# The second LayerNorm of token groups 1 to 3 moved behind attention, and transposed values copied in pairs on ScalarE

## The chip, the cores and the metric

The kernel runs on one core of one Trainium2 chip. The metric is the device time of one execution in microseconds (us); for the kernel before, three runs gave 694.21, 695.79 and 697.62, and their median is the time to compare with. The profile is that of one further execution.

## The reference

The input x is 16 batches of 128 rows of 512. It is first changed by cross-attention to a context of the same shape, then by a feed-forward with routed experts, each behind a LayerNorm over the 512 columns:

```
def _layernorm(x, axis=-1, eps=1e-05):
    m = jnp.mean(x, axis=axis, keepdims=True)
    v = jnp.var(x, axis=axis, keepdims=True)
    return (x - m) / jnp.sqrt(v + eps)
...
qk = jnp.einsum('bhdq,bhdl->bhql', qh, kh) * scale        # 8 heads of 16 rows, 512 x 512 scores
sm = jax.nn.softmax(qk, axis=-1)
ret = jnp.einsum('bhql,bhdl->bhdq', sm, vh)
...
x = x + jnp.tanh(g_xattn[0]) * xattn(_layernorm(x), ctx_2048, ctx_2048, gamma)
x = x + jnp.tanh(g_ffn[0]) * ffn(_layernorm(x), ...)
```

The feed-forward brings each of the 2048 rows down to 256 columns, picks two of eight experts by router logits on the same normalised row, adds a shared expert, goes back up to 512 columns and adds gelu(row) times a 512 x 512 core matrix. The second LayerNorm, in front of it, is the one that moves.

## The kernel before

**Attention** runs in windows, one batch begun in each. For every window TensorE computes the 512 x 512 scores of eight heads twice: once with queries on the partitions (`nat`, 16 pairs of products, from which VectorE takes row maxima with a 1.2 us reduction each, `mx`), and once with keys on the partitions (`ring`, three banks, from which ScalarE takes the exponentials, 32 instructions `P`). A small row of maxima per half of the heads is transposed and put back as one more row of the queries (`mrow`). TensorE then multiplies values and exponentials into `pv`; the value tile `VT` holds for each head 32 columns, 16 with the values and 16 with ones, so that the sums for the softmax come out of the same products. Even heads have the values first, odd heads the ones. ScalarE copies `pv` to `U` twice in a window, once per half of the heads. The values come from the context by four transposes into a ring bank, two to a bank; ScalarE copies each bank into VT with two instructions of 128 elements a partition, one for even and one for odd heads (line 661).

**After the products**, GpSimd separates numerator and denominator (lines 740 to 746), the denominator goes to memory and back (VectorE's `recip`), and GpSimd multiplies and adds the residual (`att`, `x1`, lines 750 and 754) in `ao`. One window later comes the second LayerNorm of that batch: VectorE's bn_stats and bn_aggr (`xstats`, `xaggr`, lines 698 and 702), placed after its ninth and tenth maxima; on GpSimd three small steps (`xnegm`, `xveps`, `xrstd`), the normalisation `u` into `un` (line 766), and `x1t`, which adds a constant row to x1 (line 769). SyncE stores `un` and `ao` to memory, and later loads four batches at once as a group.

**The feed-forward** handles four groups of four batches. The order on every engine is written out by hand, by `seq`. For group r TensorE transposes the normalised rows (`uT`), computes router logits (`lg`, `lt`), `h`, the token ranks (`rk`), transposes the halves of gelu(h) into rows (`rt`, from `gh` and its low part `gl`), transposes the gate table `Gp` (`gt`), and computes the core product of the group before (`core`), which stands between these. VectorE splits operands into high and low halves (`ul`, `gl`, `gul`), selects experts, and builds `Gp` from the chain csum, carry, rk, pk, slf, slots, gat, pk, Gp. ScalarE does the gelus and casts. GpSimd issues eight scatter DMAs a group (`sc`) and, from group 2 on, computes the first `gl`. An instruction waits behind all that stands before it on its engine. Four EH banks go round; a bank is free when its reader is done. The normalised rows lie in `XA` for groups 0, 1 and 3, in `u` for group 2. The last batches' LayerNorm (batch 15) runs as `last_stats` and `last_norm` inside the feed-forward.

Behind group 3 come the experts' blocks, TensorE products from end to end, and the sums.

## Time and profile before

| | |
|---|---|
| median of 3 runs | 695.79 us |
| the profiled execution | 693.51 us, of it the span 690.6 us |
| PE busy | 651.6 us, 94% of the span |
| ACT busy | 531.1 us, 77% |
| DVE busy | 515.6 us, 75% |
| POOL busy | 468.1 us, 68% |
| granted TensorE clock | full in all 40 slices |
| second LayerNorm, statistics (L698) | 16 of 680 ns |
| second LayerNorm, normalisation (L766) | 16 of 766 ns |
| value copies (L661) | 64 of 269 ns |

PE is TensorE, DVE VectorE, ACT ScalarE, POOL GpSimd, SP SyncE; L661 is line 661 of the kernel. Busy time overlaps between engines, and averages over stages with different limits, so what counts is which engine has no idle time in the stage that is changed. Of small pipelined instructions the start of the next may come before the end of the last; the pace is then the distance of starts and not the duration.

### The profile page before, as it was taken

The page shows a single profiled execution, that of the slowest core. Times are in us where ns is not written, and L with a number is a line of the kernel's source. Part 1 is how long each engine was busy: PE and PEld are TensorE (multiplying, and loading weights), DVE is VectorE, ACT ScalarE, POOL GpSimd, SP SyncE. Part 2 cuts the span into 40 slices and gives each one's busy share as a digit, 9 for nine tenths or more (in the row PEclk, how much of TensorE's full clock was granted, in tenths as well). Part 3 has the DMA queues.
Part 4 walks back from the last instruction along what each step waited for, and adds up shares of the span by engine and source line. Part 5 has one row for each costly group of instructions (what it writes and reads, how often), then busy time and mean ns, then how long its engine had stood idle before and what let it go on. Part 6 is the DMA issues. An engine that isn't in the chain of part 4 may idle for free.

```text
span 690.6 us, 18438 instructions
## 1 busy us (share of the span) xinstructions
PE 651.6 (94%) x6005; PEld 342.6 (50%) x6005; DVE 515.6 (75%) x859; ACT 531.1 (77%) x1125; POOL 468.1 (68%) x468
## 2 busy tenths in 40 slices
PE   1799999999999999999999999989999999999998
PEld 0122222222222222222345655579999998998744
DVE  3989999999999999999789877853444434444466
ACT  2389999999999999999888568567777776776411
POOL 3688898888888879986737443506756656665722
PEclk9999999999999999999999999999999999999999
DMA  6755776666767666656335653579988998696596
GB/s 195 249 168 195 221 242 199 194 187 189 221 197 228 198 180 202 190 173 210 113 123 170 228 190 123 171 166 173 125 146 116 127 130 109 99 122 91 61 299 252
DMA packets 128482, 120.40 MB, mean 174 GB/s; under 512 B 64132, under 2 KB 97668, under 8 KB 128392
## 3 DMA queue, kind: packets, MB, share of 16 engines
q1 hardware_dynamic: 114968, 104.09, 53.5%
q0 software_dynamic: 12192, 14.16, 13.7%
q8 instruction: 52, 0.85, 0.5%
q10 hardware_dynamic: 1232, 0.98, 0.5%
q14 instruction: 38, 0.31, 0.1%
HBM read 60.25 MB, written 49.10 MB: 158 GB/s over the span
## 4 chain that ended last, share of the span: by engine, by line
PE 65%; DMA 13%; POOL 11%; DVE 4%; ACT 3%; issue 2%; SPq 2%; POOLq 0%; DVEq 0%
PE EH L1333 23%; PE Y L1333 15%; PE pv L571 11%; PE ring L558 7%; PE nat L546 4%; DMA QS<-q_scratch 2%; DMA q_scratch<-qhl 2%; ACT P L642 2%; POOL wlo L812 1%; DMA u<-in_wall 1%; DMA rd<-den_scratch 1%; DMA QS<-mrow 1%; DMA k_scratch<-khl 1%; POOL y_sums L2235 1%; DMA x_rows<-ao 1%
## 5 line engine op out<-in xcount | busy, mean ns | idle before, releaser
L717 DVE TENSOR_REDUCE mx<-nat 128x2 f32<-128x1024 f32 x256 | 296.6, 1212 | 14.1 <-PE nat L546 13.8
L642 ACT ACTIVATE P<-ring 128x512 f32<-128x512 f32 x512 | 281.1, 601 | 16.8 <-PE ring L558 10.9
L2235 POOL DMA_INDIRECT y_sums<-ysb,to x74 | 124.8, 1687 | 81.6 <-DVE ysb L2165 62.5
L571 PE MATMUL pv<-P,VT 128*32 128x256 f32 x2048 | 157.6, 391 | 0.4
L546 PE MATMUL nat<-KS,QS 48*128 48x512 f16 x512 | 113.1, 394 | 20.2 <-DMA QS<-q_scratch 14.0
L558 PE MATMUL ring<-QS,KS 49*128 49x512 f16 x512 | 119.3, 391 | 9.1 <-ACT P L642 6.8
L1333 PE MATMUL EH<-XA,whi 128*128 128x256 f16 (+1 forms) x688 | 104.9, 258 | 0.5 <-DMA XA<-g_rows 0.5
L1333 PE MATMUL Y<-whi,u 128*128 x592 | 104.3, 273 | 0.2
L571 PEld LDWEIGHTS pv<-P,VT 128*32 128x32 f32 x2048 | 43.9, 108 | 99.1 <-issue 49.1
L2115 DVE TENSOR_TENSOR u<-X,u 128x512 f16<-128x512 f32 x62 | 42.7, 689 | 62.1 <-ACT u L1739 59.0
L558 PEld LDWEIGHTS ring<-QS,KS 49*128 49x128 f16 x512 | 30.7, 93 | 111.1 <-ACT P L642 88.5
L1333 PE MATMUL EH<-XA,wlo 128*128 128x256 f16 (+1 forms) x344 | 84.6, 258 | 0.0
L1333 PE MATMUL Y<-wlo,u 128*128 x296 | 80.7, 273 | 0.0
L1733 ACT ACTIVATE X<-EH,bcur 128x256 f32<-128x256 f32 x124 | 63.2, 560 | 15.7 <-PE EH L1333 8.6
L1333 PEld LDWEIGHTS EH<-XA,whi 128*128 x688 | 64.0, 98 | 7.1 <-issue 1.0
L1333 PEld LDWEIGHTS Y<-whi,u 128*128 128x128 f16 x592 | 57.9, 98 | 7.8 <-issue 1.2
L1739 ACT CAST u<-X 128x512 f16<-128x512 f32 x62 | 38.3, 618 | 5.2
L546 PEld LDWEIGHTS nat<-KS,QS 48*128 48x128 f16 x512 | 26.5, 95 | 29.2 <-issue 15.0
L1333 PEld LDWEIGHTS EH<-XA,wlo 128*128 x344 | 33.6, 98 | 2.8
L750 POOL TENSOR_TENSOR ao<-tn,rd 128x512 f32<-128x512 f32 x16 | 20.4, 1275 | 16.5 <-DMA rd<-den_scratch 16.4
L1333 PEld LDWEIGHTS Y<-wlo,u 128*128 128x128 f16 x296 | 28.9, 98 | 3.2
L1747 ACT CAST uh<-Y 128x256 f16<-128x256 f32 x16 | 6.0, 373 | 31.0 <-PE Y L1582 31.0
(282 smaller groups left out, 1039.2 us busy)
## 6 DMA issues: line engine op xcount, KB each, us to landing
QS<-q_scratch SPq DMA_DIRECT2D x64, 96.0 KB, 2.7
KS<-k_scratch SPq DMA_DIRECT2D x62, 96.0 KB, 2.3
u<-in_wall SPq DMA_DIRECT2D x7, 640.0 KB, 4.0
X<-in_x SPq DMA_DIRECT2D x16, 256.0 KB, 3.3
q_scratch<-qhl SPq DMA_DIRECT2D x16, 256.0 KB, 2.2
xr<-in_x SPq DMA_DIRECT2D x16, 256.0 KB, 3.5
rd<-den_scratch SPq DMA_DIRECT2D x16, 256.0 KB
u_rows<-un SPq DMA_DIRECT2D x16, 256.0 KB
```

The lines of the kernel that those rows point to most:

```text
L546: m = pe.matmul(nat[k % 2][:, a, :], QS[i][r, g, n, q0:q0 + P], KS[i][r, g, n, :], start=True, stop=True)
L558: pe.matmul(ring[place[key] % 3][:, :], KS[i][r, g, n, lb * P:lb * P + P], QS[i][r, g, n, :], start=True, stop=True).then_inc(t_ring.sem, 1)
L571: m = pe.matmul(pv[32 * j:32 * j + 32, q], VT[i][:, lb, g, j, :], Pb[4 * (s % 2) + j][:, q], start=(lb == 0 and half == 0), stop=(lb == 3) ...
L642: act.activation(Pb[4 * (s % 2) + j][:, :], bank[:, :], ACT.Exp).then_inc(t_use.sem, 1)
L717: dve.tensor_reduce(mx[:, k // 8, :, k % 8], nat[k % 2][:, :, :], AX.X, ALU.max).then_inc(t_max.sem, 1)
L750: done(pool.tensor_tensor(ao[i][:, :], tn[:, :], rd[:, :], ALU.mult))
L812: done(pool.tensor_tensor(wlo[:, cols], wst[i][:, 0:many], whi[:, cols], ALU.subtract))
L1333: m = pe.matmul(dst, l, r, start=first and n == 0, stop=last and n == 2, skip_group_check=skip)
L1733: m = act.activation(af[j % 2][:, tile, :], EH[j % 2][:, n, s * BLK:(s + 1) * BLK], ACT.Gelu, bias=bcur[:, j % 2, tile:tile + 1], scale=bc ...
L1739: act.copy(ah[j % 2][:, 2 * n:2 * n + 2, :], af[j % 2][:, 2 * n:2 * n + 2, :]).then_inc(t_ah.sem, 1)
L2115: dve.tensor_tensor(al[j % 2][:, 2 * n:2 * n + 2, :], af[j % 2][:, 2 * n:2 * n + 2, :], ah[j % 2][:, 2 * n:2 * n + 2, :], ALU.subtract).th ...
L2235: pool.indirect_dma_start(out=ysum[:, :], out_offset=bass.IndirectOffsetOnAxis(ap=to[:, j % 2, a:a + 1], axis=0), in_=ysb[j % 2][:, a, :], ...
```

## The change

It has two parts.

**Values.** VT becomes two stretches of 512 + 16 columns, one for even and one for odd heads. In both the values stand at the start of each 32 columns, with ones behind. The weights of an odd head are read from 16 columns further left, so that ones come first and values after; the first 16 of these lie in the spare columns at the end of the even stretch. One copy with the same pattern for both can then move a whole bank, 256 elements a partition.

**Second LayerNorm.** For batches 0 to 3 nothing changes. For batches 4 to 15 attention only computes x1 and the row with the constant added (which goes to `un` now); SyncE stores x1 itself where the normalised rows went. In the feed-forward VectorE takes statistics of a loaded group (four bn_stats, four bn_aggr) and GpSimd normalises it in place (three small steps on all four batches, four normalisations); TensorE waits for the normalisation of each batch before transposing it.

```diff
     def dve_small(w):
...
-               ([(w - 3, "xstats"), (w - 3, "xaggr")] if w >= 3 else []) + \
+               ([(w - 3, "xstats"), (w - 3, "xaggr")] if 3 <= w < 3 + G4 else []) + \
...
         if w >= 3:
-            jobs += [(w - 3, n) for n in ("xnegm", "xveps", "xrstd", "u", "x1t")]
+            if w < 3 + G4:
+                jobs += [(w - 3, n) for n in ("xnegm", "xveps", "xrstd", "u")]
+            jobs.append((w - 3, "x1t"))
...
-                ck.wait(t_pool, s, "u")
-                sp.dma_start(us[s], un[:, :]).then_inc(t_us.sem, 16)
+                ck.wait(t_pool, s, "u" if s < G4 else "x1")
+                sp.dma_start(us[s], un[:, :] if s < G4 else ao[s % 2][:, :]).then_inc(t_us.sem, 16)
...
-                        m = pe.matmul(pv[32 * j:32 * j + 32, q], VT[i][:, lb, g, j, :], Pb[4 * (s % 2) + j][:, q],
+                        m = pe.matmul(pv[32 * j:32 * j + 32, q], values(i, g, lb, j), Pb[4 * (s % 2) + j][:, q],
...
-                    src = bank[:, 0:2 * P].rearrange("p (l j g d) -> p l g j d", l=2, g=2, d=DH)
-                    for g in range(2):
-                        m = act.copy(VT[i][:, 2 * a:2 * a + 2, g, :, DH * g:DH * g + DH], src[:, :, g, :, :])
-                    m.then_inc(t_use.sem, 1)
+                    src = bank[:, 0:2 * P].rearrange("p (n g d) -> p n g d", g=2, d=DH)
+                    act.copy(value_rows[i][:, 2 * QUADS * a:2 * QUADS * a + 2 * QUADS, :, :], src).then_inc(t_use.sem, 1)
...
+        def row_stats(r):
+            wait(dve, t_uu[r % 2], r)
+            for t in range(G4):
+                if r > 1:
+                    wait(dve, t_mv, r - 1, t)
+                dve.bn_stats(sx[:, t, :], ub[r][:, t, :]).then_inc(t_sx.sem, 1)
+            for t in range(G4):
+                wait(dve, t_sx, r, t)
+                if t == 0 and r > 1:
+                    wait(dve, t_ln, r - 1, "veps")
+                dve.bn_aggr(mv[:, t, :], sx[:, t, :]).then_inc(t_mv.sem, 1)
...
+            row_stats(1)
...
-                    if o == (1, "r", "ms"):
-                        ends["late"]["vector"]()
+                    if o == (1, "gl", 1):
+                        row_stats(2)
+                    elif o == (0, "core", G4 - 1):
+                        row_stats(3)
...
+        def normed(r):
+            wait(pool, t_mv, r, G4 - 1)
...
+            for t in range(G4):
+                pool.tensor_scalar(ub[r][:, t, :], ub[r][:, t, :], ln[:, t, 0:1], ln[:, t, 2:3], ALU.add, ALU.mult).then_inc(t_nu.sem, 1)
...
+            normed(1)
...
                     elif o == (0, "sc", G4 - 1):
                         last_norm()
+                        normed(2)
+                    elif o == (1, "sc", G4 - 1):
+                        normed(3)
```

Three places in the feed-forward where the order changes. First VectorE at the first group's `gl`. Before:

```order
L1824 SCALAR_TENSOR_TENSOR red<-red 128x4
L698 BN_STATS statx<-ao 128x6
L702 BN_AGGR mvx<-statx 128x2
L2013 TENSOR_TENSOR gl<-gf,gh 128x512
L1857 TENSOR_SCALAR gat<-red 128x4
L1859 TENSOR_SCALAR gat<-red 128x4
L1865 TENSOR_TENSOR pk<-m,gat 128x32 x2
L1869 COPY Gp<-cst 128x4
L1875 TENSOR_TENSOR Gp<-pk 128x12x8
L2013 TENSOR_TENSOR gl<-gf,gh 128x512
```

And now (`ro` is the memory that holds the statistics, `XA` the rows of group 1):

```order
L1836 SCALAR_TENSOR_TENSOR red<-red 128x4
L2072 BN_STATS ro<-XA 128x6 x4
L2077 BN_AGGR mv<-ro 128x2 x4
L2025 TENSOR_TENSOR gl<-gf,gh 128x512
L1869 TENSOR_SCALAR gat<-red 128x4
L1871 TENSOR_SCALAR gat<-red 128x4
L1877 TENSOR_TENSOR pk<-m,gat 128x32 x2
L1881 COPY Gp<-cst 128x4
L1887 TENSOR_TENSOR Gp<-pk 128x12x8
L2025 TENSOR_TENSOR gl<-gf,gh 128x512
```

One bn_stats and one bn_aggr of batch 14 are replaced by four and four of group 1.

Then VectorE in group 1, from the second `gl` to the gates. Before:

```order
L1821 TENSOR_REDUCE red<-pp 128x4
L1824 SCALAR_TENSOR_TENSOR red<-red 128x4
L2013 TENSOR_TENSOR gl<-gf,gh 128x512
L1835 TENSOR_REDUCE csum<-msum 128x8
L1838 TENSOR_TENSOR carry<-carry,csum 128x8
L1841 TENSOR_TENSOR rk<-EH,cst 128x32
L1848 TENSOR_TENSOR pk<-rk,m 128x32 x2
L1851 TENSOR_REDUCE slf<-pk 128x8
L1854 CAST slots<-slf 128x8
L1857 TENSOR_SCALAR gat<-red 128x4
L1859 TENSOR_SCALAR gat<-red 128x4
L1865 TENSOR_TENSOR pk<-m,gat 128x32 x2
```

And now:

```order
L1833 TENSOR_REDUCE red<-pp 128x4
L1836 SCALAR_TENSOR_TENSOR red<-red 128x4
L2025 TENSOR_TENSOR gl<-gf,gh 128x512
L2072 BN_STATS ro<-u 128x6 x4
L2077 BN_AGGR mv<-ro 128x2 x4
L1847 TENSOR_REDUCE csum<-msum 128x8
L1850 TENSOR_TENSOR carry<-carry,csum 128x8
L1853 TENSOR_TENSOR rk<-EH,cst 128x32
L1860 TENSOR_TENSOR pk<-rk,m 128x32 x2
L1863 TENSOR_REDUCE slf<-pk 128x8
L1866 CAST slots<-slf 128x8
L1869 TENSOR_SCALAR gat<-red 128x4
```

The statistics of group 2 stand between `gl` and `csum`; those of batch 15, which stood some ten instructions further up, are gone.

Then GpSimd, from batch 15's LayerNorm to the first `gl` that it computes. Before:

```order
L2183 DMA g_rows<-XB,slots 17664x272 x4
L757 TENSOR_SCALAR lnx<-mvx 128x1
L759 TENSOR_SCALAR lnx<-mvx 128x1
L762 TENSOR_TENSOR lnx<-lnx,cst 128x1
L766 TENSOR_SCALAR un<-ao,lnx 128x512
L769 TENSOR_TENSOR ao<-ao,tb 128x512
L2183 DMA g_rows<-rows,slots 17664x272 x4
L2183 DMA g_rows<-acc,slots 17664x272 x4
L2192 TENSOR_TENSOR gl<-gf,gh 128x512
```

And now:

```order
L771 TENSOR_TENSOR un<-ao,tb 128x512
L2235 TENSOR_SCALAR ln<-mv 128x4
L2236 TENSOR_SCALAR ln<-mv 128x4
L2238 TENSOR_TENSOR ln<-ln,cst 128x4
L2241 TENSOR_SCALAR u<-u,ln 128x512 x4
L2208 DMA g_rows<-rows,slots 17664x272 x4
L2208 DMA g_rows<-acc,slots 17664x272 x4
L2235 TENSOR_SCALAR ln<-mv 128x4
L2236 TENSOR_SCALAR ln<-mv 128x4
L2238 TENSOR_TENSOR ln<-ln,cst 128x4
L2241 TENSOR_SCALAR XA<-XA,ln 128x512 x4
L2217 TENSOR_TENSOR gl<-gf,gh 128x512
```

Batch 15 keeps only its addition; group 2 is normalised ahead of the eight scatters of group 1, and group 3 between these and `gl` of group 2.

## Rows read from the trace of the kernel before

**Rows 1.** The head of the page.

```profile
span 690.6 us, 18438 instructions
```

**Rows 2.** Busy time by stretch; columns: stretch, then length, then us busy of each engine.

```profile
200.00:220.00 20.00, 19.53 (x202) 5.58 (x198) 19.76 (x23) 19.39 (x41) 17.89 (x23) 1.00 0.68 206
...
380.00:420.00 40.00, 40.00 (x257) 23.09 (x255) 29.77 (x97) 24.68 (x49) 17.58 (x19) 1.00 0.57 201
```

**Rows 3.** ScalarE in time, one attention window: start us, duration us, line, operation [idle before].

```profile
195.86 0.58 ACT L620 COPY U<-pv 128x512 f32<-128x512 f32 x1
...
200.88 0.43 ACT L661 COPY VT<-ring 128x128 f32<-128x128 f32 x2 [0.16 <-PE ring L590]
...
206.13 0.58 ACT L620 COPY U<-pv 128x512 f32<-128x512 f32 x1
...
209.77 6.14 ACT L642 ACTIVATE P<-ring 128x512 f32<-128x512 f32 x11 [0.15 <-PE ring L558]
215.81 0.58 ACT L620 COPY U<-pv 128x512 f32<-128x512 f32 x1
```

**Rows 4.** VectorE in time, the same window.

```profile
207.30 0.68 DVE L698 BATCH_NORM_STATS2 statx<-ao 128x6 f32<-128x512 f32 x1
...
209.01 0.17 DVE L702 BATCH_NORM_AGGREGATE mvx<-statx 128x2 f32<-128x6 f32 x1
```

**Rows 5.** ScalarE in time, an early window.

```profile
45.29 0.58 ACT L620 COPY U<-pv 128x512 f32<-128x512 f32 x1
...
54.97 0.58 ACT L620 COPY U<-pv 128x512 f32<-128x512 f32 x1
```

**Rows 6.** Groups by line and form, whole span; busy us, mean ns of one.

```profile
L620 ACT COPY U<-pv 128x512 f32<-128x512 f32 x32 | 18.6, 580 | 0.3 <-PE pv L571 0.3
...
L661 ACT COPY VT<-ring 128x128 f32<-128x128 f32 x64 | 13.9, 269 | 8.5 <-PE ring L590 8.5
...
L766 POOL TENSOR_SCALAR un<-ao,lnx 128x512 f32<-128x512 f32 x16 | 12.2, 766 | 1.8
```

**Rows 7.** Around the first group's gl: VectorE, then TensorE.

```profile
359.26 1.09 DVE L2013 TENSOR_TENSOR gl<-gf,gh 128x512 f16<-128x512 f32 x1 [0.42 <-ACT red L1648]
...
362.13 0.69 DVE L2013 TENSOR_TENSOR gl<-gf,gh 128x512 f16<-128x512 f32 x1
...
363.96 0.27 PE L1414 MATMUL Y<-id,gl 128*128 128x128 f16 x2
...
369.58 0.39 PE L1333 MATMUL EH<-gh,whi 128*128 128x512 f16 x1 [1.55 <-ACT uh L1608]
```

**Rows 8.** Before Gp of group 1: GpSimd, VectorE, TensorE.

```profile
381.09 0.25 POOL L757 TENSOR_SCALAR lnx<-mvx 128x1 f32<-128x1 f32 x1
...
382.41 0.78 POOL L766 TENSOR_SCALAR un<-ao,lnx 128x512 f32<-128x512 f32 x1
383.27 1.26 POOL L769 TENSOR_TENSOR ao<-ao,tb 128x512 f32<-128x512 f32 x1
...
383.34 1.35 DVE L1848 TENSOR_TENSOR pk<-rk,m 128x32 f32<-128x32 f32 x2
...
385.65 0.26 DVE L1875 TENSOR_TENSOR Gp<-pk 128x96 f32<-128x96 f32 x1
...
386.16 0.60 PE L1431 MATMUL EH<-cst,Gp 128*96 128x128 f32 x4
```

**Rows 9.** Around gl of group 2: GpSimd, VectorE, TensorE.

```profile
405.73 1.16 POOL L2192 TENSOR_TENSOR gl<-gf,gh 128x512 f16<-128x512 f32 x1
...
407.90 0.20 DVE L1835 TENSOR_REDUCE csum<-msum 128x8 f32<-128x32 f16 x1
...
408.44 0.29 DVE L1848 TENSOR_TENSOR pk<-rk,m 128x32 f32<-128x32 f32 x2
...
409.70 0.26 DVE L1875 TENSOR_TENSOR Gp<-pk 128x96 f32<-128x96 f32 x1
...
409.18 0.28 PE L1414 MATMUL Y<-id,gl 128*128 128x128 f16 x2
```

More of the change, by code:

```diff
@@ L196, in program @@
             "rbb": sb("rbb", [P, G4, E]), "tb": sb("tb", [P, L]), "lp": sb("lp", [P, L]),
+            "mv": sb("mv", [P, G4, 2]), "ln": sb("ln", [P, G4, 3]),
             "gb": sb("gb", [P, NT]), "zs": sb("zs", [P, LAT]), "Z": sb("Z", [P, LAT]),
@@ L233, in stacks @@
         if i:
-            A("gap", [P, 3, L])
+            A("gap", [P, 3 * L - 4 * DH])
         own = [A(f"{n}{i}", [P, 2, QUADS // 2, L], F16) for n in ("QS", "KS")]
-        return own + [A(f"VT{i}", [P, LB, 2, QUADS, 32])]
+        return own + [A(f"VT{i}", [P, 2, L + DH])]
     pair = [stacks(0)]
@@ L243, in attention @@
     QS, KS, VT = zip(*pair)
+    value_rows = [v[:, :, 0:L].rearrange("p g (n c) -> p n g c", c=32)[:, :, :, 0:DH] for v in VT]
+    values = lambda i, g, lb, j: VT[i][:, :, :].rearrange("p g c -> p (g c)")[:, L * g + 32 * (QUADS * lb + j):L * g + 32 * (QUADS * lb + j) + 32]
     mx = A("mx", [P, 2, 2, 8])
@@ L515, in last_x1 @@
             sp.wait_ge(t_pool.sem, t_pool.at[B - 1, "x1t"])
-            sp.dma_start(x1s[B - 1], ao[(B - 1) % 2][:, :]).then_inc(t_st.sem, 16)
+            sp.dma_start(x1s[B - 1], un[:, :]).then_inc(t_st.sem, 16)
         def last_u():
-            sp.wait_ge(t_pool.sem, t_pool.at[B - 1, "u"])
-            sp.dma_start(us[B - 1], un[:, :]).then_inc(t_us.sem, 16)
+            sp.wait_ge(t_pool.sem, t_pool.at[B - 1, "x1"])
+            sp.dma_start(us[B - 1], ao[(B - 1) % 2][:, :]).then_inc(t_us.sem, 16)
         late["sync"] = last_x1, last_u
@@ L722, in body @@
                 small(ck, *job)
-        def last_stats():
-            for what in ("xstats", "xaggr"):
-                small(Clock(dve), B - 1, what)
-        late["vector"] = last_stats
         over_windows(dve, body, tail)
@@ L741, in job @@
             elif what == "nb":
-                ck.wait(t_st, b - 2)
+                ck.wait(t_st if b - 2 < G4 else t_us, b - 2)
                 done(pool.tensor_scalar(ao[i][:, :], U[1][:, :], cme[:, 1:2], 1.0, ALU.mult, ALU.mult))
@@ L767, in job @@
             elif what == "x1t":
-                ck.wait(t_pool, b, "u")
-                done(pool.tensor_tensor(ao[i][:, :], ao[i][:, :], keep["tb"][:, :], ALU.add))
+                ck.wait(t_pool, b, "u" if b < G4 else "x1")
+                if b == G4:
+                    ck.wait(t_us, b - 1)
+                elif b > G4:
+                    ck.wait(t_st, b - 1)
+                done(pool.tensor_tensor((ao[i] if b < G4 else un)[:, :], ao[i][:, :], keep["tb"][:, :], ALU.add))
             elif what == "negm":
@@ L832, in last_norm @@
         def last_norm():
-            for what in ("xnegm", "xveps", "xrstd", "u", "x1t"):
-                job(Clock(pool), B - 1, what)
+            job(Clock(pool), B - 1, "x1t")
         def last_rows():
@@ L913, in ffn @@
     uf = A("uf", [P, LB, L])
+    mv, ln = keep["mv"], keep["ln"]
     gbs = u[:, :, :].rearrange("p t q -> p (t q)").bitcast(F16)
@@ L933, in ffn @@
     ro, wo, bo, eo = (A(n, [P, NJ], I32) for n in ("ro", "wo", "bo", "eo"))
+    sx = ro[:, 0:6 * G4].bitcast(F32).rearrange("p (t c) -> p t c", t=G4)
     bcur = A("bcur", [P, 2, 8])
@@ L998, in ffn @@
     scattered = lambda r, i: t_sf[i - 2] if r == 0 and i >= 2 else t_sc[i]
+    t_sx, t_mv, t_ln, t_nu = T("f_row_stats"), T("f_row_mean"), T("f_row_scale"), T("f_normed")
     t_zr = T("zero_rows", 16)
@@ L1068, in ffn @@
                 tally.plan(*o)
+    for r in range(1, NG):
+        for t in range(G4):
+            for t_ in (t_sx, t_mv, t_nu):
+                t_.plan(r, t)
+        for what in ("negm", "veps", "rstd"):
+            t_ln.plan(r, what)
     for r in range(NG):
@@ L1373, in do @@
             if name == "uT":
-                if i == 0:
-                    wait(pe, t_uu[r % 2], r)
                 for t in range(G4):
+                    if i == 0 and r == 0:
+                        wait(pe, t_uu[0], r)
+                    elif i == 0:
+                        wait(pe, t_nu, r, t)
                     m = pe.transpose(dst[:, t * P:t * P + P], ub[r][:, t, i * P:i * P + P], ident)
@@ L2166, in collect @@
                               ALU.mult).then_inc(t_dve.sem, 1)
-        return {(B - 2, "recip"): set_up, (B - 2, "xstats"): select_0, (B - 1, "recip"): low_0}, rest
+        return {(B - 2, "recip"): set_up, (B - 1, "recip"): low_0}, rest
     def gpsimd(pool):
@@ L2204, in some @@
             return run
+        def normed(r):
+            wait(pool, t_mv, r, G4 - 1)
+            if r > 1:
+                wait(pool, t_nu, r - 1, G4 - 1)
+            pool.tensor_scalar(ln[:, :, 0], mv[:, :, 0], -1.0, None, ALU.mult).then_inc(t_ln.sem, 1)
+            pool.tensor_scalar(ln[:, :, 1], mv[:, :, 1], EPS, None, ALU.add).then_inc(t_ln.sem, 1)
+            wait(pool, t_ln, r, "veps")
+            pool.tensor_tensor(ln[:, :, 2], ln[:, :, 1], cst[:, K_PH:K_PH + 1].broadcast_to([P, G4]), ALU.pow).then_inc(t_ln.sem, 1)
+            wait(pool, t_ln, r, "rstd")
+            for t in range(G4):
+                pool.tensor_scalar(ub[r][:, t, :], ub[r][:, t, :], ln[:, t, 0:1], ln[:, t, 2:3], ALU.add, ALU.mult).then_inc(t_nu.sem, 1)
         def output_bias():
@@ L2242, in rest @@
                 pool.tensor_tensor(*summands(n), ALU.add).then_inc(t_pool.sem, 1)
-        return {(2, "whi"): output_bias, (B - 3, "xnegm"): some(("uhp", 0), ("uhp", 1)),
+        return {(2, "whi"): output_bias, (B - 3, "x1t"): some(("uhp", 0), ("uhp", 1)),
                 (B - 2, "att"): some(("uhp", 2), ("uhp", 3))}, rest
```

7 lines of the change are left out of this document (3 added, 4 removed).

## The prediction

> **What bounds the kernel now.** I read the page first: the profiled execution took 693.51 us, a span of 690.6 [rows 1] and 2.9 us around it; the median of the three runs shown is 695.79, 2.3 above. I work in microseconds added to or taken from the span and put them on the median at the end. Then the busy time by stretch [rows 2]. Up to about 336 us the kernel is attention, in windows of 20 us, and three engines are nearly full in each: VectorE 19.76, TensorE 19.53, ScalarE 19.39 of 20, GpSimd 17.89. From 380 to 420 (groups 0 to 2 of the feed-forward) TensorE is busy for 40.00 of 40.00 at full clock, VectorE for 29.77, GpSimd for 17.58.
>
> So each half of the kernel needs its own question. In attention: which of three engines sets the window? The copies of the value sums, U, come 10.27 and 9.68 us apart (195.86, 206.13, 215.81) [rows 3], two halves of one window of 19.95. ScalarE's steady pace is eleven exponentials in 6.14 us, each 0.60 long: (6.14 - 0.60) / 10 = 0.554 from start to start. Each half has sixteen, 8.86 us. The shorter half has besides them U, one small row of maxima and the wait of 0.15, 0.82 in all. The longer one has two pairs of value copies more, 4 x 0.16 = 0.64 (0.43 for a pair, 0.27 for one copy, so the second starts 0.16 behind the first), and it is 0.59 longer. ScalarE alone explains the window to 0.1 us. VectorE idles only 0.24 us in 20, so it is close behind. The witness against it is an early window, where VectorE has no second LayerNorm yet: the half that later carries these steps lasts 54.97 - 45.29 = 9.68 us there too [rows 5]. With less to do, VectorE didn't make it shorter.
>
> In the feed-forward TensorE runs in a fixed order without a gap, so a step that reaches it late adds its lateness to the end.
>
> **What attention gains.** A line through 0.16 us for 128 elements and 0.554 for 512 puts the start-to-start time of one copy of 256 at 0.29, against 0.32 for the pair: 0.03 of engine time. By its end, a line through 269 and 580 ns [rows 6] gives 0.37 against 0.43, so TensorE is released 0.06 sooner. With 32 pairs that is 1.0 to 1.9 us, hidden by nothing where ScalarE sets the pace; I take 1.4. The ends are 0 (as many elements and one start fewer, so no loss) and 32 x 0.16 = 5.1, as if the second copy went free. The new places of the values keep runs of 16, and the products still read 32 columns in a row: nothing for either.
>
> The Trainium skill, "ScalarE: Activation LUTs" (section on table sets), gives an ACTIVATE 186 ns plus 0.833 ns an element. By an estimate from that page, with nothing overlapped, merging would save 186 ns a pair, 6.0 us in all. The rows disagree: the second copy starts 160 ns behind the first, hardly more than its elements alone.
>
> VectorE loses one statistics step and one aggregation in each of nine windows (batches 4 to 12), 0.68 and 0.17 us [rows 4]. By the witness this is worth nothing; at most it closes ScalarE's two waits for TensorE, 0.16 and 0.15 [rows 3], so 9 x 0.31 = 2.8. I take 0.4, for windows that run uneven. GpSimd loses three small steps and a normalisation a window, but it idled 2.1 us there already: nothing. SyncE still stores two rows per batch at the same place in its queue, the first now unnormalised and ready earlier: nothing. For attention that is -1.8, ends -1.0 and -7.9.
>
> **What the feed-forward pays.** The work comes back in three blocks. On VectorE a block is four statistics and four aggregations, 4 x 0.68 and 4 x 0.1 or so (small independent steps start closer than they last), 3.1 us. On GpSimd it is three small steps, 1.3 us (381.09 to 382.41 [rows 8]), and four normalisations of 0.77 [rows 6], 3.1 us.
>
> A second cost rides on that. Small VectorE steps stretch while GpSimd runs a wide one: the pair pk took 1.35 us beside x1t, which began at 383.27 and ended at 384.53 [rows 8], and 0.29 where GpSimd was idle [rows 9]; gl took 1.09 beside two wide steps and 0.69 later [rows 7]. The statistics took 0.68 beside anything.
>
> The Trainium skill states this in "SBUF — State Buffer" (the single rule and its consequences): a VectorE instruction with two SBUF inputs, or in a two-port mode, is shut out for the whole length of the GpSimd instruction. The trace agrees: pk ended just after x1t. Were the two engines independent, place 2 below would be about 2 us cheaper.
>
> *Place 1, before group 1.* VectorE's block stands ahead of group 0's first gl, in the place of one statistics step with its aggregation (0.8) and a wait of 0.42 [rows 7]: gl is 3.1 - 0.8 - 0.4 = 1.9 us late. Its stretching (0.4) falls away, since what ran beside it is over by then. The second gl ended at 362.82 and moves to 364.3, or 364.8 with x1t now beside this chain. TensorE took it at 363.96, so it is 0.5 to 1.0 late there. GpSimd's block, 4.4 us behind the statistics and x1t, ends at about 367.5; TensorE idled 1.55 us up to 369.58 anyway, after the transposes that read the block, which covers most of this. I take +1.2; ends 0 and 3. What hides the rest of the block is that idle time, gone if the rows of group 1 land late.
>
> *Place 2, group 1.* The block stands between the second gl and the chain rk, pk ... Gp. TensorE needs Gp at 386.16 and Gp ends at 385.91 [rows 8]: slack 0.25. The block adds 3.1. Batch 15's own statistics leave (0.8), and so does the stall of pk, 1.35 - 0.29 = 1.1, because x1t of batch 15 no longer waits for a norm and comes earlier. That is +1.2. But GpSimd's four normalisations now start 1.3 us after the aggregation, and the chain from csum to Gp is 409.96 - 407.90 = 2.06 us long undisturbed [rows 9]: its last 0.8 us, five or six small steps, meet four instructions of 0.77. Held up by one it is +0.8, by all four +3.1; I take the middle, +1.9. Late by 3.1, less 0.25, is +2.8; ends 1.2 and 5. Queued behind on VectorE are the rest of the chain, the table rows for the scatters and the residual sums that free TensorE's banks; all move with it.
>
> *Place 3, group 2.* GpSimd's block for group 3 stands between the last scatter of group 1 and its gl of group 2. That gl ran from 405.73 to 406.89 and TensorE takes it at 409.18 [rows 9], slack 2.3. Adding 1.3 + 3.1 makes it end at 411.3, or 411.5 with a stall: +2.3; ends 1.5 and 3.5. VectorE's own block for group 3 stands ahead of steps that TensorE reads later; 0 taken, and the upper end covers it.
>
> Feed-forward: 1.2 + 2.8 + 2.3 = +6.3, ends 2.7 and 11.5. Nothing behind absorbs it: group 3 and the expert blocks start from what came late. Together 6.3 - 1.8 = +4.5: 698.0 for an execution like the profiled one, 695.79 + 4.5 = 700.3 on the median.
>
> **The rivals.** *Heavier stalls*: each normalisation lets only one or two VectorE steps through; place 2 costs 5, the others 2 and 3.5, so 10.5 - 1.5 = +9, 705. For it: pk waited out the whole instruction beside it. Against: Gp's chain may be half done before the first one starts. *Half hidden*: Gp escapes nearly all four (1.2), place 1 costs nothing, place 3 1.5: 2.7 - 1.8 = +0.9, 697. For it: only 0.8 us of the chain is exposed. *Attention was held by VectorE together with ScalarE*: with both lighter the waits of 0.16 and 0.15 close in all 16 windows (5.0) besides the copies (1.4), against 2.7 paid: -3.7, 692. It decides once a window shortens by more than 6.3 / 16 = 0.4 us. For it: VectorE is the busiest engine there. Against: the early half of 9.68. The page's fixed cost, -6.0 against +6.3, would give no change, 696; it changes a chance little, since the 0.16 speaks against it, and it sits with the half-hidden case.
>
> **Numbers.** A measurement here can tell about 0.5%, 3.5 us, from no change. My forecast 0.50, three quarters of it beyond +3.5; heavier stalls 0.17; half hidden 0.18; faster attention 0.15, nearly all beyond -3.5. Slower: 0.38 + 0.17 = 0.55. Same: 0.12 + 0.18 + 0.01 = 0.31. Faster: 0.14. The range, 692.5 to 706, leaves out the tails of the first and the third rival; the likeliest case's own is 697.5 to 703.
>
> **What would show it.** U's 19.85 to 19.9 us apart instead of 19.95, and one value copy of about 370 ns. VectorE's idle time in a window up by 0.7. TensorE late or idle before it transposes gl of group 0 (1 us), before Gp of group 1 (2 to 4, held by VectorE) and before gl of group 2 (2, held by GpSimd). VectorE steps of 0.17 us stretched to 0.5 and more beside the normalisations. A window under 19.6, or TensorE still full from 380 to 420, would prove me wrong.

## The result and the profile after

The changed kernel took 700.32 us in the median of 14 runs (698.76 to 703.77), the kernel before 695.6 (14 runs beside it, 692.8 to 699.6): ratio 1.0078, 95% interval 1.0062 to 1.0095. It is slower by 0.8%, about 5.4 us by that ratio; the medians lie 4.7 us apart, the means 5.5. One of the twelve runs of experiment 11, 819.83 us at a granted clock of 0.763, is left out of all figures.

The profiled executions lie further apart than that: 701.86 us against 693.51, spans of 698.7 and 690.6. A difference of 8.1 us between two traces can't be explained with a cause worth 5.4. So every instruction is placed from a common point, and it is asked where the gap opens. First the busy time by stretch after (columns as in [rows 2]: TensorE, its weight loads, VectorE, ScalarE, GpSimd).

```profile
200.00:220.00 20.00, 19.53 (x200) 5.64 (x198) 19.01 (x20) 19.01 (x38) 15.52 (x18) 1.00 0.67 199
380.00:420.00 40.00, 35.42 (x233) 19.97 (x231) 31.46 (x108) 21.37 (x42) 27.60 (x29) 1.00 0.53 179
```

TensorE did 40.00 us of 40.00 in the second stretch before [rows 2], and 35.42 now: 4.6 us of idle time have appeared there. In the first stretch VectorE, ScalarE and GpSimd all have less to do, and TensorE exactly as much: 19.53.

**Attention.** ScalarE after, one window (start us, duration us):

```profile
216.46 0.58 ACT L625 COPY U<-pv 128x512 f32<-128x512 f32 x1
...
219.79 0.37 ACT L665 COPY VT<-ring 128x256 f32<-128x256 f32 x1
...
221.48 0.37 ACT L665 COPY VT<-ring 128x256 f32<-128x256 f32 x1 [0.16 <-PE ring L595]
...
226.73 0.58 ACT L625 COPY U<-pv 128x512 f32<-128x512 f32 x1
...
236.41 0.58 ACT L625 COPY U<-pv 128x512 f32<-128x512 f32 x1
```

The copies of the value sums are 10.27 and 9.68 us apart, to the hundredth as in [rows 3]. One copy of 256 elements took 0.37 us, as forecast, but from its start to the start of what follows (exponentials at 220.14 and 221.79) it takes 0.35 and 0.31 us. The pair of before took 0.34 and 0.32 (rows of experiment 12 below). The 0.06 us by which a copy ends sooner has bought nothing. The wait of 0.16 for TensorE is there still. The trace of before already held a hint at which engine matters here, in a view that the forecast didn't use: the chain of work that ended last, followed back from the last instruction, of which this is the part from 196 to 236 us, two windows:

```profile
by line: PE pv L571 44.2%; PE ring L558 29.0%; PE nat L546 15.2%; ACT P L642 4.5%; PE ring L590 2.9%; PE ring L581 2.1%; issue 1.6%; ACT U L620 1.5%
```

TensorE carries 93% of it, ScalarE 6%, and the value copies (L661) don't appear in it. Experiments 12 and 13 test this.

**Feed-forward.** The table gives, for one execution each, the time from the start of the last U copy of attention to five of TensorE's instructions: the ranks of groups 1, 2 and 3 (L1429, `EH<-msum`; L1417 before) and the transposes of Gp (L1443; L1431 before) of groups 1 and 2; groups are counted from 0. The last column is the rest, from the ranks of group 3 to the end.

```
                     ranks 1   Gp 1   ranks 2   Gp 2   ranks 3    rest
before                 21.34   28.40    47.29   54.35    73.23   259.6
after                  21.81   29.19    50.01   59.90    78.78   261.6
lateness                0.47    0.79     2.72    5.55     5.55
```

Read as steps: 0.47 before group 1, 0.32 more up to Gp of group 1, 1.93 more between there and the ranks of group 2, 2.83 more before Gp of group 2, nothing more up to group 3. The sum, 5.55 us, is 0.80% of the time, which agrees with the measured ratio. The other 2.5 us between the two traces are not the change's: the rest, which is the same code in all kernels, took between 259.2 and 261.6 us in eleven traces (these two, and runs 1 to 6 and 9 to 11 below), and the last U of attention stood at 357.8 before and 358.3 after, between 357.6 and 358.8 in the eleven. Single steps scatter too: the ranks of group 2 came 2.72 us late in this trace, 2.41 and 2.46 in those of runs 2 and 3, which are the same up to there in the feed-forward. A step of 0.3 us in the table is at that limit.

The steps in TensorE's rows after (in square brackets the idle time before, and what ended it):

```profile
365.03 0.27 PE L1426 MATMUL Y<-id,gh 128*128 128x128 f16 x2 [0.50 <-DVE gl L2025]
...
368.43 1.64 PE L1389 MATMUL EH<-cst,XA 128*128 128x128 f32 x13 [0.42 <-POOL XA L2241]
370.78 0.39 PE L1343 MATMUL EH<-gh,whi 128*128 128x512 f16 x1 [0.71 <-ACT uh L1620]
...
387.48 0.61 PE L1443 MATMUL EH<-cst,Gp 128*96 128x128 f32 x4 [0.15 <-DVE Gp L1887]
...
398.98 0.39 PE L1343 MATMUL EH<-gh,whi 128*128 128x512 f16 x1 [1.75 <-ACT uh L1620]
...
415.16 0.27 PE L1426 MATMUL Y<-id,gh 128*128 128x128 f16 x2 [2.67 <-issue]
```

*Place 1.* TensorE waits 0.50 for VectorE's gl and 0.42 for GpSimd's normalised rows; the wait of 1.55 for ScalarE that followed before [rows 7] shrinks to 0.71 in return.

*Place 2.* VectorE, then GpSimd, after:

```profile
382.60 2.46 DVE L2072 BATCH_NORM_STATS2 ro<-u 128x6 f32<-128x512 f32 x4
384.99 0.36 DVE L2077 BATCH_NORM_AGGREGATE mv<-ro 128x2 f32<-128x6 f32 x4
385.27 0.17 DVE L1847 TENSOR_REDUCE csum<-msum 128x8 f32<-128x32 f16 x1
...
385.78 0.32 DVE L1860 TENSOR_TENSOR pk<-rk,m 128x32 f32<-128x32 f32 x2
...
387.07 0.26 DVE L1887 TENSOR_TENSOR Gp<-pk 128x96 f32<-128x96 f32 x1
```

```profile
383.69 1.27 POOL L771 TENSOR_TENSOR un<-ao,tb 128x512 f32<-128x512 f32 x1
...
386.10 1.06 POOL L2238 TENSOR_TENSOR ln<-ln,cst 128x4 f32<-128x4 f32 x1
387.27 3.55 POOL L2241 TENSOR_SCALAR u<-u,ln 128x512 f32<-128x512 f32 x4
```

The block takes 2.67 us (382.60 to 385.27). It stands beside x1t (L771), beside which pk took 1.35 us before [rows 8]: pk is back to 0.32 us. And the power of -1/2 for four columns took 1.06 us where one column took 0.57 before, so the first normalisation began at 387.27, after Gp had begun. The chain from csum to the end of Gp is 2.06 us long, the undisturbed length of [rows 9]: none of the four normalisations slowed it.

*The step that I took as 0.* VectorE's block for group 3, and ScalarE behind it:

```profile
394.42 2.46 DVE L2072 BATCH_NORM_STATS2 ro<-XA 128x6 f32<-128x512 f32 x4
...
397.08 2.46 DVE L2028 TENSOR_TENSOR gul<-uf,guh 128x512 f16<-128x512 f32 x4
```

```profile
397.85 0.59 ACT L1617 COPY uf<-EH 128x512 f32<-128x512 f32 x1 [1.86 <-DVE gul L2028]
```

gul, the low halves of group 1, reads the buffer uf. ScalarE may write group 2's columns there only after that, and TensorE's first product of group 2 waits for ScalarE's copies to free the banks they stand in: 1.75 us. The chain is VectorE to ScalarE to TensorE, through a buffer that is freed, not through a value that is needed. I had followed only the values.

*Place 3.* GpSimd after:

```profile
409.04 0.24 POOL L2235 TENSOR_SCALAR ln<-mv 128x4 f32<-128x4 f32 x1
...
409.68 1.04 POOL L2238 TENSOR_TENSOR ln<-ln,cst 128x4 f32<-128x4 f32 x1
410.83 3.11 POOL L2241 TENSOR_SCALAR XA<-XA,ln 128x512 f32<-128x512 f32 x4
413.90 1.15 POOL L2217 TENSOR_TENSOR gl<-gf,gh 128x512 f16<-128x512 f32 x1
```

gl begins at 413.90 instead of 405.73 [rows 9]; 4.86 us of that is the block (409.04 to 413.90), the rest is what GpSimd was late before it. Three steps of VectorE beside the normalisations were stretched as forecast, pk to 0.66 and 0.70 us and Gp to 0.72, but TensorE wasn't waiting for them: it stands for 2.67 us until gl is done at 415.05. (The trace names no releaser; the end of gl is 0.11 us ahead.)

### The profile page after: what moved, and what is told of

The parts are those of the page before. It is cut to its first block and busy times, and to the rows that moved or that the text cites. A ratio compares the mean times of both kernels' runs of the same rounds, so it can differ in the third digit from the quotient of the medians.

```text
span 698.7 us, 18374 instructions
## 1 busy us (share of the span) xinstructions
PE 654.9 (94%) x6005; PEld 342.8 (49%) x6005; DVE 514.5 (74%) x859; ACT 530.5 (76%) x1093; POOL 462.2 (66%) x441
## 5 line engine op out<-in xcount | busy, mean ns | idle before, releaser
L1727 ACT ACTIVATE X<-EH,bcur 128x128 f32<-128x128 f32 x48 | 18.1, 456 | 14.9 <-PE EH L1343 14.9
```

The costliest lines, as they stand in the source:

```text
L1727: m = act.activation(af[j % 2][:, tile, 0:P], EH[j % 2][:, 0, tile * P:(tile + 1) * P], ACT.Gelu, bias=bcur[:, j % 2, tile:tile + 1], scal ...
```

## The experiments

Two theories went into them. *Theory A*: attention gained nothing, and the loss is the feed-forward's stalls, each a term of its own. *Rivals*: the value copies did gain or lose something; the stalls hide one another; VectorE beside GpSimd, and not the order on the engines, is what costs. All ratios are to runs of the kernel before on the same chip. What a run gains over the changed kernel is the difference of two such ratios, and uncertain by 1.6 to 1.9 us; the traces are finer.

### 1 and 2: the two halves of the change alone

`e1_values_only` is the kernel before with the value copies of the change and their layout; `e2_norm_only` the changed kernel with the old ones. The edit of the first:

```diff
-                    src = bank[:, 0:2 * P].rearrange("p (l j g d) -> p l g j d", l=2, g=2, d=DH)
-                    for g in range(2):
-                        m = act.copy(VT[i][:, 2 * a:2 * a + 2, g, :, DH * g:DH * g + DH], src[:, :, g, :, :])
-                    m.then_inc(t_use.sem, 1)
+                    src = bank[:, 0:2 * P].rearrange("p (n g d) -> p n g d", g=2, d=DH)
+                    act.copy(value_rows[i][:, 2 * QUADS * a:2 * QUADS * a + 2 * QUADS, :, :], src).then_inc(t_use.sem, 1)
```

> The kernel before, with the new layout of the transposed values and the single value copy alone; the second LayerNorm stays where it was. Theory A (the trace of the changed kernel: start to next start of the single copy 0.35 and 0.32 us, as of the old pair): no change, 695.6 +- 1 us, window still 19.95 us. Rival B (my forecast's term): attention shorter by 1.4 us, 694.2. Rival C (the saving is hidden by some other limit of the changed kernel and only shows here): shorter by more, each window by the 0.16 us of one instruction, about 693.

> The changed kernel with the old pair of value copies and the old layout: only the LayerNorm of groups 1 to 3 is moved. Theory A: the whole loss is in the move, so 700.3 +- 1 us as the changed kernel, windows of 19.95 us. Rival B: without the single copy attention is longer by 1.4, 701.7 us. Rival C: the new layout itself costs (a read with a stride, the shifted half), then this one is faster than the changed kernel.

Measured: 695.08 us, ratio 1.0003 (0.9982 to 1.0025), and 701.14 us, ratio 1.0086 (1.0063 to 1.0110). The value copies are worth nothing that can be told, in either kernel; the loss is in the move. The interval of the first alone reaches down to -1.25 us, just short of the forecast's -1.4; its trace has windows of 10.27 and 9.68 us, as before, and the ranks of group 3 stand 73.22 us behind the last U, against 73.23.

### 3: the low half of group 2 ahead of the normalisation

```diff
-                    elif o == (1, "sc", G4 - 1):
+                    elif o == (2, "gl", 0):
                         normed(3)
```

> The changed kernel with one move on GpSimd: group 3's normalisation is issued behind the low half of the hidden values of group 2, not ahead of it. Theory A: the low half comes at about the time it had before, the transposes of L1426 in group 2 no longer wait 2.67 us, so 2.8 us shorter: 697.5 us. Rival B: VectorE's small steps there are slowed by the normalisation on GpSimd wherever it stands beside them (pk 0.66, Gp 0.72 instead of 0.29, 0.26), and these are what TensorE waits for: then half or less comes back, 699 us or more.

Measured: 697.01 us, ratio 1.0021 (1.0004 to 1.0038), where the changed kernel has 1.0078: 4.0 us come back. GpSimd in this run:

```profile
408.65 1.17 POOL L2217 TENSOR_TENSOR gl<-gf,gh 128x512 f16<-128x512 f32 x1
...
412.25 3.54 POOL L2241 TENSOR_SCALAR XA<-XA,ln 128x512 f32<-128x512 f32 x4
```

TensorE's row has no wait at L1426 of group 2 any more, and the ranks of group 3 stand at 75.69 instead of 78.78, 3.09 us sooner. Of that, 0.27 is there at Gp of group 1 already, ahead of the step that was moved, and is scatter; 2.82 is the move's, which is place 3 (2.83) whole. Theory A holds; rival B would have left half. That the runs gained 4.0 is within their uncertainty; the clock, below, may have a part in it.

### 4: the statistics of group 3 in VectorE's gaps

`stats_of` and `means_of` are the two loops of `row_stats`.

```diff
-                    elif o == (0, "core", G4 - 1):
-                        row_stats(3)
+                    elif o == (0, "core", G4 - 2):
+                        stats_of(3, range(3))
+                    elif o == (2, "ul", 0):
+                        stats_of(3, range(3, G4))
+                    elif o == (2, "ul", 3):
+                        means_of(3)
```

> The changed kernel with group 3's statistics taken apart on VectorE: three of the four bn_stats in the gap of 1.84 us before the last core step of group 0, the fourth behind the first ul of group 2, the four bn_aggr behind the last ul. The normalisation stays where it was. Theory A: the block of 2.8 us ahead of the guls made ScalarE's uf copy wait 1.86 us and TensorE 1.75; that goes, so 1.9 us shorter: 698.4 us. Rival B: the stall at GpSimd's low half of group 2 comes later anyway and takes up what is won here (the normalisation starts at the scatter before it, not at the statistics): no change, 700.3 us.

Measured: 698.80 us, ratio 1.0053 (1.0032 to 1.0074): 1.7 us back, which the runs alone could not tell from nothing; 1.62 in the trace (ranks of group 3 at 77.16), 1.43 of it behind Gp of group 1. VectorE, then ScalarE:

```profile
392.69 1.88 DVE L2076 BATCH_NORM_STATS2 ro<-XA 128x6 f32<-128x512 f32 x3 [0.80 <-DMA XA<-u_rows]
```

```profile
395.93 0.59 ACT L1617 COPY uf<-EH 128x512 f32<-128x512 f32 x1
```

ScalarE's wait of 1.86 us is gone, and with it TensorE's 1.75. Of the 1.93 us of this step 0.50 stay. 0.27 of them are at a new place: the three statistics wait 0.80 us for the rows of group 3 to land, so the core step behind them is late and TensorE waits for it at its transposes. Where the rest lies was not followed up. The stall at place 3 is there in full, 2.67 us. It didn't take up what was won, so rival B falls.

### 5, 6 and 11: both moves, and group 1 left in attention

Run 5 has the two edits above. Run 6 is the changed kernel with the bounds `G4` of the phase in attention put to `2 * G4`, and without `row_stats(1)` and `normed(1)`; run 11 has all three.

> The changed kernel with both moves: group 3's normalisation behind GpSimd's low half, and group 3's statistics in VectorE's gaps. Theory A (two stalls at two places, one behind the other on TensorE's path): they add up, 3.3 + 1.5 us off 700.3, so 695.5 us, what is left over the kernel before is group 0's and 1's 0.5 to 1 us. Rival B (one stall takes up the other's gain): no better than the better of the two, 697.

> The changed kernel with the LayerNorm of group 1 (iterations 4 to 7) left in attention as before; only groups 2 and 3 are moved, at their places of the changed kernel. Theory A: the stall at the first low half and the first transposes of group 1 (rt +0.65, then 0.5 to 0.7 us kept) goes, nothing changes in attention, whose windows are 19.95 us with and without: 699.7 us. Rival B (my forecast's size): 1.2 us shorter, 699.1. Rival C: attention pays for the VectorE and GpSimd work of four more iterations: 700.5 or more.

> Both moves of group 3, and group 1's LayerNorm left in attention. Theory A (all stalls are separate terms on TensorE's path): 695.85 less 0.8 is 695.0 us, as the kernel before. Rival B: ScalarE's wait at the uf copies of group 1 takes up what is won (1.55 us at the first product in place of 0.71 when only group 1 was kept): 695.9.

Measured: run 5 695.85 us, ratio 1.0007 (0.9987 to 1.0027); run 6 699.49 us, 1.0057 (1.0038 to 1.0077); run 11 695.36 us (median of eleven), 1.0010 (0.9996 to 1.0025). The lateness against the kernel before, from the traces, in the same terms as above:

```
                     ranks 1   Gp 1   ranks 2   Gp 2   ranks 3    ratio
after                   0.47    0.79     2.72    5.55     5.55   1.0078
3 low half first        0.47    0.52     2.46    2.46     2.46   1.0021
4 statistics in gaps    0.31    0.60     1.10    3.93     3.93   1.0053
5 both                  0.31    0.56     1.31    1.31     1.32   1.0007
6 group 1 kept         -0.13    0.11     2.04    4.87     4.87   1.0057
11 all three           -0.13    0.13     1.42    1.43     1.43   1.0010
```

Two stalls one behind the other on TensorE's path add up. Counted from Gp of group 1 on, run 3 brings 2.82 us and run 4 1.43, 4.25 together; run 5 with both brings 4.00. The 0.25 between them is what TensorE waits more for the late rows at the new place, 0.52 us instead of 0.27. With both moves the LayerNorm's move is free within what the runs can tell; the trace still has 1.32 us, so the two places in two engines' rows were 4.2 of its 5.55 us. Leaving group 1 in attention brings 0.68 us in the trace alone, and nothing behind the two moves, where TensorE then waits 1.07 us for the core step held up by the same late rows. So place 1's size is 0.5 to 0.7 us by the traces. The runs gained 1.5 in run 6, which can't be told from the forecast's 1.2.

### 7, 9 and 10: a value copy given to VectorE

If ScalarE sets the window, VectorE's free time ought to be worth a copy. From iteration 7 on one of the two copies goes to VectorE, behind its max number k (counted from 0): run 7 the first copy behind k = 3, on the changed kernel; run 9 the second behind k = 3 and run 10 the first behind k = 2, both on run 5. TensorE, which waited for the second copy before its first product with the values, now waits for both, in every window.

```diff
-                            ck.wait(t_use, b, "vt", 1)
+                            for a in range(2):
+                                ck.wait(t_vc if moved((b, "vt", a)) else t_use, b, "vt", a)
...
                         small(ck, *todo.pop(0))
+                    if k == 3 and moved((w, "vt", 0)):
+                        ck.wait(t_ring, w, "vt", 0)
+                        dve.tensor_copy(value_rows[w % 2][:, ...], ring[...][:, 0:2 * P]...).then_inc(t_vc.sem, 1)
```

> The changed kernel with the first of the two value copies of each iteration from 7 on given from ScalarE to VectorE, behind its fourth max. Theory A: ScalarE sets the window (32 exps, 2 sums, 2 value copies, max rows; 19.95 us) and VectorE has 0.69 us to spare a window since the LayerNorm's bn_stats and bn_aggr are gone: the window gets shorter by the copy's 0.33 us, nine windows, 3 us: 697.3 us. Rival B: VectorE holds the window too (busy 19.0 to 19.8 of 20 us in the rows): the copy stands between two maxes and TensorE waits, windows of 19.95 or more: 700.3 or slower. Rival C: TensorE itself (19.5 us busy of 20) is the floor, about half of it: 698.8.

> The kernel of the last call with both moves (695.85 us), and from iteration 7 on the second value copy on VectorE right behind its fourth max, where VectorE waited 0.26 us for the next scores anyway. In the run before, the first copy stood one max too late: the transposes of the second value pair waited 1.08 us for its bank (TensorE L597). Theory A: with no such wait, ScalarE's 0.33 us a window comes off nine windows: about 3 us shorter, 692.8 us, windows of about 19.6 us. Rival B: VectorE holds the window too, with any copy on it the maxes fall behind: 695.9 or more. Rival C: TensorE is the floor at 19.5 busy of 19.95: half of it, 694.4.

> As the run above, but the first value copy, behind VectorE's third max (one max earlier than in the run that took 711.8 us). Theory A (only the bank's wait made that run slow): 1.1 us a window come back and ScalarE's 0.33 with them: 692.8 us. Rival B (any copy on VectorE between two maxes delays TensorE): still several us over 695.9. If this one and the run above differ, the place in VectorE's row decides, not its load.

Measured: 711.82 us, ratio 1.0223 (1.0191 to 1.0256); 696.08 us, 1.0021 (1.0004 to 1.0038); 695.79 us, 1.0011 (0.9990 to 1.0032). Run 7 is slow for the reason in its row of TensorE, the bank that VectorE still held; nine half windows of 11.55 instead of 10.27 us make 11.5 us, which is what it has over the changed kernel:

```profile
228.27 0.44 PE L597 MATMUL ring<-cst,X 128*128 128x128 f32 x2 [1.08 <-DVE VT L729]
```

But runs 9 and 10, without that wait, gained nothing over run 5. The time of run 9 is what its rival B named, 695.9 or more, but not for B's reason: VectorE itself waits for TensorE in such a window, 0.38 us at 209.01. ScalarE in run 9:

```profile
221.41 5.03 ACT L651 ACTIVATE P<-ring 128x512 f32<-128x512 f32 x9 [0.48 <-PE ring L564]
```

The time of the copy turned into a wait for TensorE of 0.48 us. Windows are 20.09 us (10.41 and 9.68), 0.14 more than before. The moved copy is not the cause, for an early window has the same 10.41 with both copies still on ScalarE:

```profile
135.54 0.58 ACT L627 COPY U<-pv 128x512 f32<-128x512 f32 x1
139.02 0.37 ACT L669 COPY VT<-ring 128x256 f32<-128x256 f32 x1
140.70 0.37 ACT L669 COPY VT<-ring 128x256 f32<-128x256 f32 x1 [0.16 <-PE ring L597]
145.95 0.58 ACT L627 COPY U<-pv 128x512 f32<-128x512 f32 x1
```

The 0.14 us stand in TensorE's row ahead of the first product with the values, which starts 0.84 us behind U (216.77) where it starts 0.69 behind it in run 5 (207.58); the edit put its second wait just there. So these two runs changed two things at once. What they do show is that taking a copy from ScalarE shortened no window, 10.41 us with it and without it. This speaks against theory A's own assumption, and my forecast's, that ScalarE sets the window; with TensorE's row lengthened by the edit it doesn't settle it. Experiment 13 does.

### 12 and 13: who sets the window

On the kernel before. Run 12 gives TensorE four more instructions a window. Run 13 takes ScalarE's value copies of iterations 2 to 15 away, and with them TensorE's waits for these; the values of iterations 0 and 1 are used again:

```diff
-                    for n in range(2):
+                    for n in (0, 1) * 2:
                         lb = 2 * a + n
```

```diff
+                if dropped(key):
+                    continue
                 bank = ring[place[key] % 3]
                 ck.wait(t_ring, *key)
```

> The kernel before, with TensorE's two transposes of every value pair issued twice into the same bank (the values stay the same): 4 more TensorE instructions an iteration, 0.11 us apart in the rows. Theory A2 (formed after the copies given to VectorE brought nothing: TensorE's own row sets the window, it has no gap but the 0.23 us behind ScalarE's exp twice a window): each iteration longer by 4 x 0.11, 16 of them, 7 us: 702.5 us. Theory A as I held it (ScalarE sets the window, TensorE has slack): under 2 us, 697 or less.

> The kernel before, with ScalarE's value copies of iterations 2 to 15 left out (four instructions an iteration; the values of iterations 0 and 1 are used again, so the output is not the reference's): 0.66 us less of ScalarE an iteration. Theory A2 (TensorE's row sets the window): no change within 1.5 us, 695 us, with the time appearing as ScalarE's waits for the ring. Theory A (ScalarE sets it): 14 x 0.66 = 9 us shorter, 686. My forecast's term rested on A.

Measured: 697.93 us, ratio 1.0062 (1.0042 to 1.0082), and 693.73 us beside 692.85, ratio 1.0013 (0.9997 to 1.0029). Without four ScalarE instructions, 0.66 us a window, the kernel is not faster: theory A wanted 9 us. Windows stay at 10.27 and 9.68 us. (The trace of run 13 is of an execution of 696.74 us, in which one half window lasted 14.49 us; it is the one under the clock below.) TensorE before, one half of a window, and the same half in run 13:

```profile
218.73 0.38 PE L590 MATMUL ring<-cst,X 128*128 128x128 f32 x2
219.07 0.56 PE L558 MATMUL ring<-QS,KS 49*128 49x512 f16 x2
...
226.24 0.39 PE L558 MATMUL ring<-QS,KS 49*128 49x512 f16 x1 [0.23 <-ACT P L642]
```

```profile
222.66 0.38 PE L593 MATMUL ring<-cst,X 128*128 128x128 f32 x2
...
230.17 0.39 PE L561 MATMUL ring<-QS,KS 49*128 49x512 f16 x1 [0.23 <-ACT P L647]
```

Both need 7.51 us from the transposes to the wait of 0.23, to the hundredth. ScalarE before had, and in run 13 lacks, the copies:

```profile
219.15 0.43 ACT L661 COPY VT<-ring 128x128 f32<-128x128 f32 x2
219.49 0.60 ACT L642 ACTIVATE P<-ring 128x512 f32<-128x512 f32 x1
...
220.83 0.43 ACT L661 COPY VT<-ring 128x128 f32<-128x128 f32 x2 [0.17 <-PE ring L590]
221.15 5.03 ACT L642 ACTIVATE P<-ring 128x512 f32<-128x512 f32 x9
```

```profile
223.43 0.60 ACT L647 ACTIVATE P<-ring 128x512 f32<-128x512 f32 x1 [0.30 <-PE ring L561]
...
225.08 5.03 ACT L647 ACTIVATE P<-ring 128x512 f32<-128x512 f32 x9 [0.48 <-PE ring L561]
```

0.30 and 0.48 us of waiting stand where the copies stood. TensorE's row sets the window, together with three short waits for ScalarE's exponentials (0.23, 0.23, and a third inside the row of 0.56 above), and the copies lie in the shadow of both. Run 12 lengthens a window by 0.23 us (U copies 10.50 and 9.68 apart, 230.70, 240.38, 250.88), 3.7 us in sixteen windows, beside 4.3 measured (2.9 to 5.7): a little over half of the 7 I expected. The third short wait took up most of the rest; in run 12 its row lasts 0.39 us instead of 0.56:

```profile
223.65 0.39 PE L558 MATMUL ring<-QS,KS 49*128 49x512 f16 x2
```

## Why the prediction was right, and where it wasn't

The forecast was 700.3 us with slower at 0.55, and the median came out at 700.32. The reason given, attention gains little and the feed-forward pays with stalls, is what experiments 1 to 6 show. The sum is better than its terms, though. In the order of this list, what was measured lies +1.4, +0.4, -0.7, -2.5, +1.9 and +0.5 us from what was forecast. That this adds up to only +1.05, and that the median came to 0.02 us, is luck:

- *Value copies, -1.4*: 0 (experiments 1, 2, 13). The line through 0.16 and 0.554 us gave 0.03 us of engine time a pair, and the rows show about none (0.35 and 0.31 for one copy, 0.34 and 0.32 for a pair). The step "hidden by nothing where ScalarE sets the pace" was wrong besides: ScalarE doesn't, as run 13 shows. Sixteen exponentials, a U and small steps do add up to a half window to 0.1 us, but that only says that ScalarE is as full as TensorE, not that it is the one waited for. The trace had the other reading: TensorE had no wait but three short ones in such a window. I had only read its busy time. The ends of attention don't follow either: the terms' own ends, 0 to 5.1 and 0 to 2.8, add up to 0 and -7.9, not -1.0 and -7.9, and what came was the 0 that the sum left out.
- *VectorE's relief, -0.4*: 0. The witness, the early half of 9.68 us [rows 5], was right on VectorE.
- *Place 1, +1.2*: +0.47, and 0.68 by the trace of experiment 6. The wait of 1.55 that was there shrank to 0.71 and so gave back 0.84 of what TensorE had lost.
- *Place 2, +2.8*: +0.32, and 0.17 and 0.05 in runs 2 and 3, so hardly more than scatter. The block is 2.67 us, not 3.1; of that 1.39 came back, since carry and pk had been stretched beside GpSimd's normalisation and x1t (I had put down 1.1); TensorE was 0.47 late there itself; and the 1.9 for normalisations met by the chain was 0, because the power step took 1.06 us and they began behind Gp. The rival "half hidden" was nearest at this place, with 1.2. My ends of 1.2 and 5 don't follow from the terms, which give 1.2 + 0.8 - 0.25 = 1.75 and 1.2 + 3.1 - 0.25 = 4.05; the measured one lies under either.
- *VectorE's block for group 3, 0*: +1.93, of which experiment 4 gave 1.43 back. "Ahead of steps that TensorE reads later" was true and not enough: one of them frees a buffer that ScalarE writes for TensorE sooner.
- *Place 3, +2.3*: +2.83 (experiment 3: 2.82 in the trace). GpSimd's block took 4.86 us where I had 4.4, by its power step of 1.04 us. The 0.2 that I had added for a stall of VectorE was not needed: TensorE waited for gl alone.

Feed-forward: forecast 6.3, traced 5.55; the whole: forecast 4.5, measured 5.4 by the ratio, 4.7 by the medians. Of the signs that I had named, the copy of 370 ns and VectorE's 0.7 us came; windows of 19.85 to 19.9 did not (19.95). The waits at the three places came with 0.9, 0.15 and 2.67 us where I had named 1, 2 to 4 and 2. VectorE's steps stretched beside the normalisations came too, at place 3, where TensorE didn't wait for them. Of the rivals, heavier stalls fell (no stretched step held TensorE up), and so did a faster attention (windows of 19.95) and a fixed cost saved with each copy (0 instead of -6.0); half hidden came nearest at places 1 and 2 only.

## What to carry to other kernels

Where three engines are 97 to 99% full, the busy time doesn't tell which one sets the pace; read the chain of releases for a few windows, look for the engine whose row has no gaps but those that another's row explains, and before any edit ask what its row would do if the other engine's step were gone. An experiment that takes that step away altogether (run 13) says more than one that moves it, which can bring a wait of its own (runs 9 and 10). When a block of work is put into an engine's queue, follow for each instruction behind it not only who reads its result but also whose buffer it sets free. An in-order queue has free places: the same 2.7 us of statistics and 4.9 us of normalisation for group 3 cost 4.8 us at one place and under 1 us a few instructions on.

## What the runs showed of the hardware

**A stall can be followed by a lower clock, and then costs TensorE more than its own length.** In the trace of run 2 the same wait as at place 3 (2.65 us) was followed by a granted clock of 0.83, 0.50 and 0.82 in the next three stretches of 2 us; 0.50 is the lower level, 1.2 GHz. The products of 512 columns then start 0.43 us apart instead of 0.22, so Gp of group 2 comes at 61.26, not 59.90 us as in the changed kernel's trace (whose clock stayed 1.00 after 2.67 us; so it did in the traces of runs 4 and 6, after 2.67 and 2.66).

```profile
414.18 0.27 PE L1426 MATMUL Y<-id,gh 128*128 128x128 f16 x2 [2.65 <-issue]
...
416.08 0.63 PE L1343 MATMUL EH<-whi,gul 128*128 128x512 f16 x1
416.51 0.63 PE L1343 MATMUL EH<-whi,guh 128*128 128x512 f16 x1
```

```profile
414.00:416.00 2.00, 1.82 (x13) 1.02 (x14) 1.60 (x6) 1.07 (x2) 0.11 (x2) 0.83 0.00 0
416.00:418.00 2.00, 2.00 (x6) 0.73 (x5) 0.00 (x0) 0.00 (x0) 1.70 (x2) 0.50 0.53 199
418.00:420.00 2.00, 2.00 (x16) 1.28 (x15) 0.00 (x0) 0.46 (x1) 0.35 (x1) 0.82 0.20 72
```

The counts point the same way. Of 40 runs of the four kernels that have this stall (the changed one, runs 2, 4 and 6) 22 had a mean clock under 1.000; of 163 runs without it (92 of the kernel before, 71 of runs 1, 3, 5, 9, 10 and 11) 49. In the changed kernel's own 14 runs, seven at 1.000 have a median of 699.97 us, seven below it 701.91. So some 0.5 us of its 5.4 may be the clock's (a quarter more of the runs, by 2 us), and that is on the side on which experiment 3 gained more than its trace shows. It is an estimate from counts, and the stall isn't shown to be what lowers the clock. Of the runs without this stall a third have a lower mean clock too, and the trace of run 13 has a place for it, an early window of attention where TensorE waits for queries to land:

```profile
78.51 0.39 PE L549 MATMUL nat<-KS,QS 48*128 48x512 f16 x2 [3.17 <-DMA QS<-q_scratch]
```

```profile
80.00:82.00 2.00, 2.00 (x16) 0.33 (x8) 1.98 (x4) 0.39 (x2) 1.92 (x4) 0.50 1.12 227
```

At the same place TensorE waited 1.50 us in run 12, and the clock fell to 0.55 and 0.59; in run 7 it waited 2.98 us and the clock stayed 1.00. The length of a wait alone doesn't decide it.

**GpSimd's power of four columns took 1.04 to 1.12 us** in all three blocks after. Of one column, in the kernel before:

```profile
381.72 0.57 POOL L762 TENSOR_TENSOR lnx<-lnx,cst 128x1 f32<-128x1 f32 x1
```

The multiplications by -1 on four columns, 0.24 and 0.25 us at 409.04 and 385.44, are as long as on one [rows 8].

**Statistics of four tiles back to back** take 2.46 us on VectorE, 0.60 apart, where GpSimd issues a scatter and adds beside them (382.60) as well as beside scatters alone (394.42), and four aggregations 0.36.
